# First attention of a two-layer transformer kernel started on the statistics of four of 32 row tiles, weights loaded between the pieces of x

## The reference, cut to what matters

```python
def _layernorm(x, axis=-1, eps=1e-05):
    m = jnp.mean(x, axis=axis, keepdims=True)
    v = jnp.var(x, axis=axis, keepdims=True)
    return (x - m) / jnp.sqrt(v + eps)
...
    q = (x @ Wq).reshape(b, n, N_HEADS, HEAD_DIM)
    k, v = jnp.split(ctx @ Wkv, 2, axis=-1)
...
    q = apply_axial_rope(q, pos_map)
    k = apply_axial_rope(k, ctx_pos_map)
    scale = 1.0 / np.sqrt(HEAD_DIM).astype(np.float32)
    logits = jnp.einsum('bqhd,bkhd->bhqk', q, k) * scale
    w = jax.nn.softmax(logits, axis=-1)
    attn = jnp.einsum('bhqk,bkhd->bqhd', w, v)
    attn = attn.reshape(b, n, N_HEADS * HEAD_DIM)
    return attn @ Wout + bout
...
x = x + _L0_xattn_ref(_layernorm(x, axis=-1), ctx_1024, ...)
x = x + _L0_ffn_ref(_layernorm(x, axis=-1), ...)
x = x + _L1_xattn_ref(_layernorm(x, axis=-1), ctx_1024, ...)
x = x + _L1_ffn_ref(_layernorm(x, axis=-1), ...)
```

## Time and profile before

| | us |
|---|---|
| median of 3 runs | 1014.71 (1013.2 to 1016.26) |
| profiled execution, its own time | 1014.0 |
| its span (first to last instruction) | 1012.0 |
| PE busy | 863.5 (85%) |
| DVE busy | 674.9 (67%) |
| ACT busy | 427.6 (42%) |
| POOL busy | 334.1 (33%) |

### The profile page before, as it was taken

The page is one execution under the profiler, slowest core; times in us unless marked ns, Lnnn a source line. Parts: engine busy times, 40 slices in busy tenths (PEclk is TensorE's granted clock), DMA queues, the critical chain, the costliest instruction groups (busy, mean ns, idle before and its releaser), DMA issues. The chain is left out here.

```text
span 1012.0 us, 25976 instructions
## 1 busy us (share of the span) xinstructions
PE 863.5 (85%) x9368; PEld 644.2 (64%) x9368; DVE 674.9 (67%) x1581; ACT 427.6 (42%) x1027; POOL 334.1 (33%) x292
## 2 busy tenths in 40 slices
PE   0799999999999899999979999999998860288883
PEld 0477777777777689898846666666665640155552
DVE  5577877777787675555467777777776489546652
ACT  1244434344443432332556666666666660022330
POOL 1444434334343031000033333333333110247763
PEclk9999999999999999999999999999999985589997
DMA  9300000000001000000001111111110199855542
GB/s 296 94 14 17 10 16 16 10 16 10 16 13 34 2 1 12 0 0 0 3 11 23 31 31 31 31 31 31 31 31 25 49 350 306 210 146 94 92 71 31
DMA packets 62074, 56.60 MB, mean 56 GB/s; under 512 B 24017, under 2 KB 57169, under 8 KB 62033
## 3 DMA queue, kind: packets, MB, share of 16 engines
q1 hardware_dynamic: 55888, 46.61, 15.8%
q0 software_dynamic: 6144, 9.44, 5.5%
HBM read 41.81 MB, written 14.22 MB: 55 GB/s over the span
## 5 line engine op out<-in xcount | busy, mean ns | idle before, releaser
L404 ACT ACTIVATE pr_t<-bank 128x512 f32<-128x512 f32 x128 | 76.4, 597 | 159.7 <-PE bank L300 158.9
L824 POOL TENSOR_TENSOR g_k_bd<-g_k_t,head_mask 128x1024 f32<-128x1024 f32 x32 | 60.6, 1893 | 134.4 <-ACT g_k_t L999 134.4
L312 PEld LDWEIGHTS bank<-v_bd,pr_t 128*64 128x64 f32 x2048 | 70.0, 137 | 26.5 <-issue 26.3
L300 PE MATMUL bank<-ident,sub 128*128 128x128 f32 x512 | 82.2, 283 | 3.6 <-ACT pr_t L404 2.9
L312 PE MATMUL bank<-v_bd,pr_t 128*64 128x18 f32 x2048 | 82.8, 214 | 0.1
L481 DVE TENSOR_TENSOR sub<-bank,top 128x2048 f32<-128x2048 f32 x32 | 73.3, 2292 | 3.9
L300 PEld LDWEIGHTS bank<-ident,sub 128*128 128x128 f32 x512 | 55.9, 141 | 30.8 <-issue 17.2
L261 POOL TENSOR_TENSOR rot<-part_a,part_b 128x512 f32<-128x512 f32 x32 | 40.7, 1273 | 103.4 <-DVE part_b L490 103.4
L477 DVE TENSOR_REDUCE top<-bank 128x32 f32<-128x2048 f32 x32 | 73.1, 2284 | 0.6 <-PE bank L288 0.4
L648 ACT ACTIVATE f_hid<-bank,b 128x128 f32<-128x128 f32 x128 | 36.5, 368 | 85.7 <-PE bank L594 85.7
L269 POOL TENSOR_TENSOR k_bd<-qk_t,head_mask 128x1024 f32<-128x1024 f32 x32 | 60.6, 1893 | 31.2 <-ACT qk_t L419 31.2
(11 more groups left out here) (203 smaller groups left out, 2001.5 us busy)
## 6 DMA issues: line engine op xcount, KB each, us to landing
e_w_gu<-in_experts_in SPq DMA_DIRECT2D x11, 768.0 KB, 10.7
table<-r_row SPq DMA_DIRECT2D x16, 320.0 KB, 8.6
e_w_d<-in_experts_out SPq DMA_DIRECT2D x11, 384.0 KB, 13.4
xres<-in_x SPq DMA_DIRECT2D x4, 1024.0 KB, 9.8
out<-xres SPq DMA_DIRECT2D x32, 128.0 KB, 1.7
xres<-in_experts_in SPq DMA_DIRECT2D x3, 768.0 KB, 19.8
keys_in<-in_ctx_t SPq DMA_DIRECT2D x32, 64.0 KB, 1.8
vals_in<-in_ctx_t SPq DMA_DIRECT2D x32, 64.0 KB, 1.8
```

Of the source, the lines that this page charges most:

```text
L300: m = pe.transpose(b_pr[:, j * P:(j + 1) * P], sub[:, v, cols], k.ident[:, :])
L312: m = pe.matmul(b_o[64 * b:64 * b + 64, hp * VW0:(hp + 1) * VW0], pr_t[:, e, j, b * S:(b + 1) * S], v_bd[:, v, b, hp, :], start=True, stop ...
L404: act.activation(pr_t[:, e, :, :].rearrange("p j q -> p (j q)"), b_pr[:, :], ACT.Exp).then_inc(a_exp, 1)
L824: pool.tensor_tensor(k_bd[:, v, :, :, :, :].rearrange("p c b h s -> p (c b) h s"), k_t[:, v, :, :].rearrange("p c (b a s) -> p (c b) a s", ...
```

## The change

x is cut at tiles 0, 4, 14, 23 and 32 instead of 0, 8, 16, 24 and 32. The piece of four tiles is issued first, then the five weight tensors and the context of tile 0, then the other three pieces, then the context of tile 1. VectorE takes the statistics of tiles 0 to 3 alone before turn 0; those of tiles 4 to 13 stand in its turn 0 between `xn` and the rotation, those of tiles 14 to 31 in the same place of turn 1. The variances of the 28 tiles are made after turn 1, their scales on ScalarE after turn 2, their shifts on VectorE after turn 3; tile 4, in turn 4, is the first to use them. TensorE waits for the weights between the transposes of `xn` and the projection of turn 0.

```diff
+PART_ENDS = (0, 4, 14, 23, NT)
...
             for dst, src in consts:
                 sp.dma_start(dst, src).then_inc(a_const, 16)
-            for c in range(PARTS):
-                load_x(c)
+            load_x(0)
             for dst, src in weights:
                 sp.dma_start(dst, src).then_inc(a_weights, 16)
             both(0, 0, 0)
+            for c in range(1, len(parts)):
+                load_x(c)
             both(1, 0, 1)
...
         def tensor(pe):
             pe.wait_ge(a_const, 16 * len(consts))
-            pe.wait_ge(a_weights, 16 * len(weights))
...
                 if on[0]:
+                    if not later(t, 1):
+                        pe.wait_ge(a_weights, 16 * len(weights))
                     pe.wait_ge(keys_done[u], 16 * (i + 1))
...
-            row_scales(act, k, OF_X)
+            row_scales(act, k, EARLY_X_SUMS, first_x)
+
+            def late_scales():
+                row_scales(act, k, LATE_X_SUMS, last_x)
...
-            for c, part_in in enumerate(x_in):
-                dve.wait_ge(part_in, 16)
-                for t in range(c * NT // PARTS, (c + 1) * NT // PARTS):
+
+            def part_statistics(c):
+                dve.wait_ge(x_in[c], 16)
+                for t in range(NT)[parts[c]]:
                     dve.bn_stats(tile_of(k.raw, t), tile_of(k.xres, t)).then_inc(a_raw, 1)
-            dve.wait_ge(a_raw, NT)
-            row_statistics(dve, k, OF_X)
-            row_shifts(dve, k, OF_X)
-            dve.wait_ge(a_table, 4)
+
+            def late_sums():
+                dve.wait_ge(a_raw, NT)
+                row_statistics(dve, k, LATE_X_SUMS, last_x)
+
+            def late_shifts():
+                row_shifts(dve, k, LATE_X_SUMS, last_x)
+
+            part_statistics(0)
+            dve.wait_ge(a_raw, PART_ENDS[1])
+            row_statistics(dve, k, EARLY_X_SUMS, first_x)
+            row_shifts(dve, k, EARLY_X_SUMS, first_x)
+            parts_ahead = {0: (1,), 1: (2, 3)}
...
+                if not later(t, 1):
+                    dve.wait_ge(a_table, 4)
+                if not later(t, 2):
+                    for c in parts_ahead[t]:
+                        part_statistics(c)
...
         def _(act):
-            a_step = a.scalar(act)
-            turns(act, a_step, NT, 5)
+            a_step, a_late_scales = a.scalar(act)
+            for n in range(3):
+                turn(a_step, NT, 5, n)
+            a_late_scales()
+            turns(act, a_step, NT, 5, 3)
...
         def _(dve):
-            a_step = a.vector(dve)
-            turns(dve, a_step, NT, 5)
+            a_step, a_late_sums, a_late_shifts = a.vector(dve)
+            for n in range(2):
+                turn(a_step, NT, 5, n)
+            a_late_sums()
+            turn(a_step, NT, 5, 2)
+            turn(a_step, NT, 5, 3)
+            a_late_shifts()
+            turns(dve, a_step, NT, 5, 4)
```

More of the change, by code:

```diff
@@ L57 @@
 EARLY_F, EARLY_G, EARLY_R = 28, 26, 26
-OF_X, EARLY_F_SUMS, LATE_F_SUMS, EARLY_G_SUMS, LATE_G_SUMS, EARLY_R_SUMS, LATE_R_SUMS = range(7)
+PART_ENDS = (0, 4, 14, 23, NT)
+EARLY_X_SUMS, LATE_X_SUMS, EARLY_F_SUMS, LATE_F_SUMS, EARLY_G_SUMS, LATE_G_SUMS, EARLY_R_SUMS, LATE_R_SUMS = range(8)
 def turn(step, tiles, depth, n):
@@ L203, in first_attention @@
         k.a_x1, k.a_raw1 = a_x1, a_raw1
-        PARTS = len(x_in)
+        parts = [slice(first, end) for first, end in zip(PART_ENDS, PART_ENDS[1:])]
+        first_x, last_x = parts[0], slice(PART_ENDS[1], NT)
         consts = [(k.ident[:, :], ins["ident"]), (freq[:, :], ins["freq2"]), (head_mask[:, :], ins["head_mask0"]),
@@ L217, in load_x @@
             def load_x(c):
-                part = slice(c * NT // PARTS, (c + 1) * NT // PARTS)
-                sp.dma_start(k.xres[:, part, :], x_rows[:, part, :]).then_inc(x_in[c], 16)
+                sp.dma_start(k.xres[:, parts[c], :], x_rows[:, parts[c], :]).then_inc(x_in[c], 16)
             def load(dst, done, used, t, i, u):
@@ L438, in step @@
                                    ACT.Copy).then_inc(a_attTc, 1)
-            return step
+            return step, late_scales
         def vector(dve):
@@ L511, in step @@
                                       ALU.mult).then_inc(a_att, 1)
-            return step
+            return step, late_sums, late_shifts
         return Stage(z.signals, sync=sync, gpsimd=gpsimd, tensor=tensor, scalar=scalar, vector=vector)
```

## The result

The changed kernel's median of 4 runs is 1007.79 us (1006.73 to 1009.01) against 1015.44 us for 4 runs of the kernel before; the ratio is 0.9928, with a 95% interval from 0.9907 to 0.9950. Forecast were 1004.7 and a range from 1001.5 to 1008.5. The changed kernel was measured twice more beside the kernel before: 0.9959 (0.9934 to 0.9984, 10 runs) and 0.9974 (0.9952 to 0.9996, 12 runs). All runs of the two kernels in these three measurements together have medians of 1010.2 (26 runs) and 1014.5 (63 runs); one run of the kernel before, at 2055.5 us in the slow state, is left out. The gain is real and nearer to 4 us than to the 9.6 of the sum, and the medians of the two later measurements, 1009.8 and 1012.1, lie above the forecast range. In the profiled executions 1014.0 became 1007.22, with spans of 1012.0 and 1005.4.

The account below looks back on a forecast made before the run. TensorE was taken to set the pace from the fourth turn on, so the ramp shifts everything: 9.9 us earlier, less 0.2 for sums and 0.1 for shifts, gains 9.6 us, giving 1004.7 us, range 1001.5 to 1008.5.

Parts of the forecast that it names:

- rival A: Whole program: the ramp moves forward as the step-by-step sum says, giving 1003.0 to 1006.5 us; chance 0.60.
- B: Turns 0 and 1: pieces of x come late and VectorE waits; 2 us late gives 1006.7 us; chance 0.12.
- C: TensorE's half-speed clock stretch moves: 1003.3 us without it, 1006.5 with a second one; chance 0.18.
- First landing 6.8, first xn 10.0: Start of ramp: four-tile piece lands at 6.8 us, first xn at 10.0 instead of 22.24; landing has 2.4 us of slack.
- The new wait for weights costs nothing: TensorE, turn 0: it waits for weights at 11.8 us, where they have lain for 1.9 us, so no cost.
- Weights and context in at 9.9, second piece at 13.7: Loads behind the first piece: weights and tile 0's context take 3.1 us, then ten tiles of x 3.76 us.
- The tie in turn 1: Turn 1: VectorE's 18 bn_stats and TensorE's 7.62 us chain both end at 24.7 us, the second rotation, instead of 34.58.
- Sums of 28 tiles 0.83 us, of which 0.2 show: VectorE ahead of the third xn: the sums take 0.83 us, of which 0.2 us lengthens the program.
- Scales and shifts: Scales, 0.6 us, fall into ScalarE's idle time at no cost; shifts, 0.23 us ahead of the fifth xn, cost 0.1.
- "From turn 3 on the old pattern, 9.6 us earlier": Turn 3 onward: a sign expected in the new profile, old timing kept and everything 9.6 us earlier.
- Slower (E): TensorE's clock stays at 1.2 GHz through turns 3 to 5 after the interrupted ramp, giving 1027 us; chance 0.04.
- no change (D): Gain doesn't last, later parts bound by their own time or pieces not overlapping; under 3 us left, 1012; chance 0.06.

Follow-up runs that it names:

- after_third: The changed kernel run again unaltered, its third measurement beside the kernel before: median 1012.1 us, ratio 0.9974.
- both: Changed kernel with tile 2's keys issued ahead of the later layers' loads and the five late sums moved behind turn 2: 1006.7 us, ratio 0.9950.
- b_order: Kernel before with only the load order changed, weights and tile 0's context behind the first piece of x: 1020.3 us, ratio 1.0051.
- wobo3: Changed kernel with tile 2's keys ahead of later loads, late sums before turn 2's rotation, output weights and bias behind x's second piece: 1005.7 us, ratio 0.9930.
- best6: Changed kernel with x in 4, 6, 9, 8, 5 tiles, statistics over turns 0 to 3, output weights, tile 1's context, tile 2's keys moved: 1004.4 us, 0.9910.
- b_keys2: Kernel before with only tile 2's keys issued ahead of the later layers' loads: 1015.4 us, ratio 1.0007.
- keys2: Changed kernel with the keys' context of tile 2 issued ahead of the later layers' loads: 1007.7 us, ratio 0.9948.

## Why the prediction was right, and where not

**The direction and the range** held: 1007.79 in 1001.5 to 1008.5. The range held in part by luck. The same kernel's medians in the two later measurements, 1009.8 and 1012.1, lie outside it, and of the first profile's 6.6 us only 2.1 were left of the ramp at 785 us. 1007.79 also lies above what rival A (1003.0 to 1006.5), B (1006.7) or C (1006.5) had each for itself. The size was off, 9.6 us forecast against 7.65 measured first and about 4 over all runs, and the sum was right at some steps and wrong at others.

**TensorE sets the pace from the fourth turn on, so a shift of the ramp shifts the program**: right as far as the feed-forward. In the six other profiles whose clock reads 1.00 from 335 to 365 us (after_third, both, b_order, wobo3, best6, b_keys2) the lead over before at the feed-forward is that at the last scores within 0.1 us. Behind it the lead changes by up to 2.2 us until 785 us and by several us in the expert stage, and that was not in the sum.

**First landing 6.8, first xn 10.0**: 6.3 and 9.25. VectorE then waited 5.67 us for the second piece, so it didn't matter, as said.

**The new wait for weights costs nothing**: right here, the wq passes of turn 0 began 1.79 us after xn, as before. In the third profile of the change there was a wait for the keys' context of 1.5 us, and it too had no effect, since VectorE waited longer for x.

**Weights and context in at 9.9, second piece at 13.7**: 11.6 and 15.3, wrong by 1.7 and 1.6 us. All of the 1.6 is on the path, for which rival B had the price and 0.12. The term that was mis-sized is the 3.1 us of the seven loads, taken from a stretch behind all of x: they took 5.3 here, 4.1 in b_order and 6.6 in the third profile, between those 3.1 and the 7.6 that the prediction named as the far end and set aside. The ten tiles behind them took 3.7, as forecast.

**The tie in turn 1**: right. Rotation to rotation is 7.60 us after (7.62 before), with 18 bn_stats in the gap and no wait for x.

**Sums of 28 tiles 0.83 us, of which 0.2 show**: wrong. 1.75 us (from 27.42 to the third xn, 29.17), because of the shared port; TensorE's wv passes, 8.4 us ahead before it and 7.5 behind it, came 0.9 us late by it. The 0.2 was also too low by its own rows: the transposes of `xn` began 0.23 us after xn was ready (36.18 to 36.41), so they would have ended at 37.68 and not at 37.45, 0.3 us behind 37.36. I had looked for such contention at the bn_stats and the clock, and not at the one place where a two-input instruction was put right behind the one that starts GpSimd.

**Scales and shifts** went as forecast: the scales stood in ScalarE's idle time (33.26 to 33.84), the shifts took 0.17 us ahead of the fifth xn.

**"From turn 3 on the old pattern, 9.6 us earlier"**: the step that failed most, and in none of the rivals. It took 3.85 - 0.97 = 2.9 us of the 4.2 lost between the second rotation (8.4 ahead) and the wq passes of turn 2 (4.2 ahead). I followed the loads that the change moves and not those that it leaves: the keys' context of tile 2 was issued at 34.38 (33.13 before), while its use moved from 40.43 to some 33.4. keys2 and b_keys2 show it from both sides. Of the rest, 0.9 us are the sums, and 0.5 wv's passes, which took 1.12 us for 0.66.

**The clock** (rival C, a stretch falling elsewhere) took part as well, and not only in the ramp. In the ramp the record's low stretch was longer, from within 30 to 31 us until within 40 to 41, where before it ran from within 39 to 40 until within 43 to 44 (mean clock 0.77 for 0.92 from 22 to 44 us). This is past the 36 us that the prediction gave as a sign of being wrong. It lay mostly over a TensorE that waited anyway, and the wq passes of turn 2 ran at the slow duration before as well; what it added are the 0.5 us of wv's passes. Later on the clock takes more than I allowed: 4.2 to 4.6 us in each of the four profiles that had a low stretch of some 13 us between 339 and 362 us. The expert stage differs by 2.8 us between two profiles of the same kernel; its cause stays open. My range had 1.5 us a side for the runs; 30 runs of the kernel before in one measurement spread over 12.

**Slower (E) and no change (D)** did not come.

## What to carry to other kernels

When a stage is pulled forward, list every transfer that its first turns use, the unmoved ones too, and compare each one's issue time on its queue with the new time of its use: a load that had 5.5 us of slack before (landed at 34.9, used at 40.43) became the bound here. Put new two-input VectorE work where GpSimd is idle, and not behind the instruction that starts GpSimd. Where runs spread by 1%, judge a change of 0.5% by starts inside the trace ahead of the spread's source, and only then by medians.

## What the runs showed of the hardware that was not expected

- A VectorE tensor_tensor with two SBUF inputs (128x28) lasts 0.20 us alone, and 1.28 us beside a GpSimd tensor_tensor of 1.28 us in seven profiles; bn_stats beside GpSimd kept 0.33 us.
- The DMA engines together fell from some 350 GB/s to between 115 and 225 in the slowest us when the 256 KB of wo and a 128 KB bias that 128 partitions read from one row came through between the first pieces of x, in all eleven profiles that had them there. The dip followed these loads to their new place, and wasn't there when they came behind all of x.
- Seven loads of 64 to 256 KB, 1024 KB in all, took 3.1 us behind 4 MB of x and 4.1, 5.3 and 6.6 us between two pieces of it.
- The granted clock stood at 0.50 for some 13 us between 339 and 362 us in four profiles, and for under 4 us or not at all from 335 to 365 us in the other ten, though TensorE had been busy 78% or more ahead of it; each long stretch took 4.2 to 4.6 us.
